# Attention scores over 32 rows per pair of heads, two units side by side, and value products for four pairs at once

## The chip, the cores and the metric

The kernel runs on one core of one Trainium2 chip. The metric is device time of one launch in microseconds (us), lower is better. PE is TensorE, PEld its weight loads, DVE is VectorE, ACT is ScalarE, POOL is GpSimd, SP is the engine that issues most transfers.

## What is computed

The reference is one layer in three parts: cross-attention, a state-space block (convolution, scan over 64 steps, gates) and a feed-forward block with rounded weights and activations. Only the first part is touched:

```python
# x: (16, 64, 256), ctx: (16, 256, 256), 16 heads of 16 columns, mask: (16, 256)
q = layernorm(x) @ Wq * 16 ** -0.5
k, v = split(ctx @ Wkv)
attn = softmax(where(mask, -inf, q_head @ k_head.T))      # per batch row and head
x = x + (attn @ v_head) @ Wproj + bproj
x = x + mamba(layernorm(x))
x = x + ffn(layernorm(x))
```

## The kernel before

The 1024 rows of x are eight tiles of 128 rows, each of two batch rows of 64. All heads are held as columns of two halves `hf` of 128 partitions, eight heads each. While tile t goes through its attention, the keys, queries and values of tile t+1 are made, and the end of tile t-1 (projection, norms) is done. All arithmetic here is float32.

A tile's attention is eight **units** (`UNITS`), and the function `body` of each engine is one pass over steps u = 0 to 7. A unit holds a bank of scores of 128 x 512: two matmuls of 256 columns each. With 64 query rows, a matmul of 128 output rows takes two heads. In the kernel before, unit u belongs to one batch row (`bb = u // 4`) and to two pairs of heads. The pairs are told apart by zeros: `spread_queries` on GpSimd writes `qbd`, in which the 128 rows hold the queries of one head and zeros for the seven others, so that each score matmul contracts over all 128 partitions (`scores`, L456).

A unit's way through the engines:

- TensorE writes its scores to bank u % 2 (`scores`; called at step u-2).
- VectorE adds the mask and takes the maximum (`mask_scores`, L1173, two instructions and two short reads of the accumulator), into one of four buffers `sm`.
- ScalarE takes the exponent (`exps`, L868), VectorE inverts the sums (`invert_sums`, L1180, one step later), GpSimd multiplies (`normalise`, L1596).
- TensorE transposes the probabilities into bank 2 or 3 (`turn_probs`, L465, at step u+1).
- ScalarE copies the even units, VectorE the odd ones, to `pt_sb` (`copy_pt`, L874 and L1185, at step u+3).
- TensorE multiplies with the values (`values`, L481), in `o_ps` with four pairs of heads in four groups of 32 columns of the array.

At step u TensorE first issues the scores of unit u+2, which wait for the mask of unit u (`masked`), so that one bank can be filled while the other is masked. Each engine works through its own list in order; a waiting instruction holds all behind it. The order is the one written in `body`: `PE_KEYS0, PE_KEYS1` and so on are the steps at which TensorE makes the first and second half of the keys (0, 2; L493), the queries (3; L509), the values of both batch rows (4, 5; L520), `project` (3; L530) and `scan_in` (6; L537). VectorE does at step 4 `pick_heads` (L1191, L1195), at step 5 `copy_keys`, `copy_queries`, `make_mask` and `add_proj`, at step 6 `norm_y1`, at step 7 `copy_vals` and `norm_z`. On every even step it copies an odd unit's probabilities.

Three tiles have more to do: in tile 5 ScalarE sums the weights' magnitudes, in tile 6 VectorE rounds the weights (L1273 and others), and in tile 7 it convolves (L1308, L1312) while TensorE does the first products of the next part. Tile 0 builds constants on VectorE at step 6 (L1281, L1282).

Of the kernel before, what the change touches and what calls it, by code (L numbers as in the profile page):

```python
# [45 lines left out]
CON_ID, CON_HEAD, CON_PAR, CON_SEL, CON_M64 = 0, 128, 136, 138, 155  # L46
# [17 lines left out]
LAG_TURN, LAG_VALUES = 1, 2  # L64
# [8 lines left out]
POOL_RSTD0, POOL_BIAS, POOL_RSTD1, POOL_RSTD2, POOL_SPREAD0 = 2, 3, 4, 6, 3  # L73
POOL_SPREAD1 = 5
# [16 lines left out]
def build(nc, x, ctx_t, mask, wq, wkv, wproj, bproj, vecs, cons, win, wall, wout, wg, wu, wd, out):  # L91
    with ExitStack() as ctx:
# [74 lines left out]
        pt_sb = first_use(13312, 2048).rearrange("p (u a q) -> p u a q", u=4, a=4)  # L167
# [6 lines left out]
        qt = first_use(24576, 256).rearrange("p (k t) -> p k t", k=KD)  # L174
# [58 lines left out]
        q_ready, q_sb = sem("q_ready", PE), sem("q_sb", DVE)  # L233
# [4 lines left out]
        qbd_ready = sem("qbd_ready", POOL)  # L238
# [52 lines left out]
        def lagged(tile, u, lag, first, fn, only=None):  # L291
# [4 lines left out]
            if only is None or v % 2 == only:  # L296
                fn(tile if v >= 0 else tile.step(-1), v % UNITS)
# [145 lines left out]
        def _(pe):  # L443
            start(pe, PE)
            def scores(tile, u):
                bb, hf, jj = u // 4, (u // 2) % 2, u % 2
                if u == 0:
                    pe.wait_ge(qbd_ready, count(tile.t * 2 + 2))
                    pe.wait_ge(k_sb[0], count(tile.t + 1))
                if u == 2:  # L450
                    pe.wait_ge(k_sb[1], count(tile.t + 1))
# [17 lines left out]
            def values(tile, u):  # L469

                bb, hf = u // 4, (u // 2) % 2
                if u == 1:
                    pe.wait_ge(v_in_sb[0], count(tile.t + 1))
                    pe.wait_ge(att_ready, count(tile.t))
                if u == 5:
                    pe.wait_ge(v_in_sb[1], count(tile.t + 1))
                pe.wait_ge(pt_in_sb[0], count(tile.t * 4 + (u // 2 + 1)))
# [1269 lines left out]
```

## Time and profile before

| | us |
|---|---|
| three runs | 557.35, 552.49, 557.58 |
| median | 557.35 |
| the profiled execution, its own time | 556.49 |
| its span | 554.7 |
| mean granted clock of TensorE | 0.94 |

In the trace a float32 matmul stands as two instructions (x4 for two matmuls), a transpose as one. The profile gives busy time for each engine, the granted clock of TensorE (1.00 is its full speed), what each instruction waited for, and the chain of work that ended last. The attention takes the span's stretch from 19 us to 226 us.

### The profile page before, as it was taken

How to read it: one execution, taken by the hardware profiler on the slowest of the kernel's cores; microseconds unless marked ns; L12 is line 12 of the kernel's file. 1: busy time of each engine (PE TensorE's matmuls, PEld its weight loads, DVE VectorE, ACT ScalarE, POOL GpSimd, SP SyncE). 2: the span in 40 equal slices, each digit the busy share in tenths (PEclk: the TensorE clock that was granted, in tenths of full speed). 3: DMA queues.
4: the chain of work that ended last, by engine and by line, in shares of the span. 5: the costliest groups of instructions: out<-in, count | busy, mean ns of one | idle time of the engine just before them, and what ended most of it. 6: DMA issues, size and time to landing. Idle time of an engine off the chain costs nothing.

```text
span 554.7 us, 9494 instructions
## 1 busy us (share of the span) xinstructions
PE 465.1 (84%) x3268; PEld 331.8 (60%) x3268; DVE 414.3 (75%) x800; ACT 258.5 (47%) x563; POOL 301.9 (54%) x310
## 2 busy tenths in 40 slices
PE   4999999999999797668796787999799988785463
PEld 2676777877767463346564555577678756462232
DVE  1476766766669797458789988688987799758993
ACT  1346546465754434580373263656772442223331
POOL 0554766648566624047664365689776789401100
PEclk9999999999999798977898898999999999799985
DMA  8910101101000000000000000000000000000000
GB/s 304 382 40 2 39 1 40 38 2 40 2 1 0 2 0 2 1 1 1 0 1 1 0 2 2 1 0 1 1 2 2 1 0 2 0 1 19 21 19 19
DMA packets 5806, 13.76 MB, mean 25 GB/s; under 512 B 768, under 2 KB 3584, under 8 KB 5248
## 3 DMA queue, kind: packets, MB, share of 16 engines
q1 hardware_dynamic: 5200, 12.67, 6.3%
q8 instruction: 26, 0.43, 0.3%
q10 hardware_dynamic: 560, 0.51, 0.3%
q14 instruction: 20, 0.16, 0.1%
HBM read 12.12 MB, written 1.05 MB: 24 GB/s over the span
## 4 chain that ended last, share of the span: by engine, by line
PE 48%; DVE 23%; issue 10%; POOL 8%; ACT 6%; DVEq 0%; ACTq 0%; POOLq 0%
PE ps L456 8%; PE ps L700 6%; PE ps L710 6%; POOL both L1652 5%; DVE both L1341 4%; PE ps L465 4%; PE ps L493 4%; PE ps L520 3%; ACT both L969 3%; PE ps L481 3%; PE ps L728 3%; DVE xc L1312 2%; PE ps L552 2%; PE ps L664 2%; DVE xc L1308 2%
## 5 line engine op out<-in xcount | busy, mean ns | idle before, releaser
L1652 POOL TENSOR_TENSOR both<-both 128x1024 f32<-128x1024 f32 x64 | 152.0, 2388 | 70.3 <-DVE both L1341 70.2
L1341 DVE TENSOR_TENSOR_SCAN both<-both,ps 128x1024 f32<-128x1024 f32 x64 | 145.1, 2280 | 33.8 <-PE ps L710 21.7
L700 PE MATMUL ps<-both 64*128 64x256 f32 x512 | 78.1, 426 | 25.4 <-DVE both L1341 17.8
L868 ACT ACTIVATE both<-both,negmax 128x256 f32<-128x256 f32 x128 | 63.8, 500 | 67.8 <-DVE negmax L1173 67.7
L969 ACT ACTIVATE both<-delta,a_neg 128x504 f32<-128x504 f32 x128 | 79.6, 705 | 25.7 <-DVE both L1341 25.7
L1596 POOL TENSOR_SCALAR both<-both,rden 128x256 f32<-128x256 f32 x128 | 63.3, 508 | 51.2 <-DVE rden L1180 51.2
L710 PE MATMUL ps<-con,both 128*128 128x128 f32 x512 | 75.6, 294 | 3.8 <-POOL both L1652 3.8
L710 PEld LDWEIGHTS ps<-con,both 128*128 128x128 f32 x512 | 59.6, 149 | 26.9 <-issue 19.1
L700 PEld LDWEIGHTS ps<-both 64*128 64x128 f32 x512 | 47.1, 197 | 45.6 <-DVE both L1341 27.8
L456 PE MATMUL ps<-both 128*128 128x256 f32 x256 | 70.1, 397 | 5.0 <-POOL both L1585 3.5
L1173 DVE CUSTOM_DVE_ANT_0 both<-ps,both 128x256 f32<-128x256 f32 x128 | 49.0, 420 | 17.3 <-PE ps L456 16.7
L456 PEld LDWEIGHTS ps<-both 128*128 128x128 f32 x256 | 45.0, 194 | 18.1 <-issue 7.2
L1585 POOL TENSOR_TENSOR both<-both,con 128x1024 f32<-128x1024 f32 x16 | 32.3, 2024 | 26.0 <-DVE both L1150 26.0
L1185 DVE COPY both<-ps 128x512 f32<-128x512 f32 x32 | 21.9, 684 | 25.7 <-PE ps L465 25.7
L465 PE MATMUL ps<-con,both 128*128 128x128 f32 x256 | 39.6, 278 | 1.0 <-ACT both L874 0.6
L465 PEld LDWEIGHTS ps<-con,both 128*128 128x128 f32 x256 | 32.4, 144 | 10.1 <-issue 4.4
L493 PE MATMUL ps<-both 128*128 128x512 f32 x64 | 32.3, 632 | 6.3 <-DMA both<-in_ctx_t 6.3
L520 PE MATMUL ps<-both 128*128 128x256 f32 x128 | 30.1, 379 | 0.0
L982 ACT ACTIVATE both<-ps 128x512 f32<-128x512 f32 x24 | 13.1, 595 | 32.9 <-PE ps L653 32.9
L1657 POOL TENSOR_TENSOR f_s<-f_s,eps 128x1 f32<-128x1 f32 x8 | 1.5, 190 | 49.0 <-DVE f_s L1411 49.0
L520 PEld LDWEIGHTS ps<-both 128*128 128x128 f32 x128 | 24.2, 190 | 3.3
L868 ACT ACTIVATION_READ_ACCUMULATOR both<-both,negmax 128x1 f32 x128 | 24.1, 188 | 0.0
(143 smaller groups left out, 704.3 us busy)
## 6 DMA issues: line engine op xcount, KB each, us to landing
both<-in_ctx_t SPq DMA_DIRECT2D x8, 512.0 KB, 3.3
both<-in_wg SPq DMA_DIRECT2D x1, 1024.0 KB, 10.4
both<-in_wu SPq DMA_DIRECT2D x1, 1024.0 KB, 12.3
both<-in_wd SPq DMA_DIRECT2D x1, 1024.0 KB, 14.3
win_sb<-in_win SPq DMA_DIRECT2D x1, 1024.0 KB, 16.8
resid<-in_x SPq DMA_DIRECT2D x1, 896.0 KB, 8.9
both<-in_wkv SPq DMA_DIRECT2D x1, 512.0 KB, 3.9
both<-in_mask SPq DMA_DIRECT2D x1, 512.0 KB, 6.0
```

The lines of the kernel that those rows point to most:

```text
L456: mm = pe.matmul(bank(u % 2)[:, q * LK:(q + 1) * LK], qbd[:, tile.par, bb, hf, j * P:(j + 1) * P], kt_sb[:, tile.par, hf, bb * LK:(bb + 1) ...
L465: tr = pe.transpose(bank(2 + u % 2)[:, (q * 2 + kt) * P:(q * 2 + kt + 1) * P], sm[:, u % 4, q * LK + kt * P:q * LK + (kt + 1) * P], ident)
L493: mm = pe.matmul(bank(6 - hf), wkv_sb[:, k, hf * P:(hf + 1) * P], ctx_sb[:, tile.par, k], start=k == 0, stop=k == KD - 1)
L520: mm = pe.matmul(bank(5 + bb)[:, kt * D:(kt + 1) * D], ctx_sb[:, tile.par, k, bb * LK + kt * P:bb * LK + (kt + 1) * P], wkv_sb[:, k, D:2 * ...
L700: mm = pe.matmul(out_v[:, :, s], ut[L * r:L * (r + 1), e.idx % 2, 2 * e.tt + s], bd[L * r:L * (r + 1), e.nh, e.tt, s * HN // 2 * L:(s + 1) ...
L710: mm = pe.matmul(bank(4 + e.idx % 2)[:, e.tt * P:(e.tt + 1) * P], h_sb[:, hu % RING_H, n * P:(n + 1) * P], ident, start=False, stop=e.nh = ...
L868: act.activation(s, s, ACT.Exp, scale=-1.0, bias=negmax[:, u % 4, q:q + 1], accum_out=den[:, u % 4, q:q + 1]).then_inc(expd, 1)
L969: act.activation(da[sl % 2].rearrange("p (a n s t) -> p a n s t", a=GT, n=HN, s=2)[:, :, n, :, 1:L], delta[:, idx % RING_X].rearrange("p ( ...
L1173: dve.tensor_tensor_reduce(sm[:, u % 4, q * LK:(q + 1) * LK], bank(u % 2)[:, q * LK:(q + 1) * LK], maskf[:, tile.par, bb * LK:(bb + 1) * L ...
L1341: dve.tensor_tensor_scan(h_sb[:, hu % RING_H], da[e.slot % 2][:, e.tt * HU:(e.tt + 1) * HU], bank(2 * (hu % 2), 2), 0.0, ALU.mult, ALU.add ...
L1596: pool.tensor_scalar(s, s, rden[:, u % 4, q:q + 1], 1.0, ALU.mult, ALU.mult).then_inc(normed, 1)
L1652: pool.tensor_tensor(h, h, cb[:, e.nh, e.tt], ALU.mult).then_inc(g_ready, 1)
```

## The change

- `q2` takes the place of `qbd` and `qt`. VectorE's `copy_queries` is now two instructions instead of one: it writes the queries twice, multiplied once by the parity column of the even heads and once by that of the odd heads (`CON_PAR`). Thus 32 partitions hold one pair of heads, and 64 + 64 columns tell its heads apart. GpSimd's `spread_queries` is gone.
- A score matmul contracts over the 32 partitions of one pair. Unit u is now one pair of heads (of half `hf = u // 4`) with both batch rows; its two matmuls are the two batch rows. `scores` is called for even u alone and issues units u and u+1 together, in turns, in different rows of the array and in banks 0 and 1. It waits until all units below u are masked (`masked`, 2u). Each of both units still has its own `s_ready`, and VectorE masks them one after the other.
- `values` is called twice a tile, for four units at once (16 matmuls instead of four times 8), with a lag of 3 steps instead of 2. `pt_sb` has eight buffers in place of four.
- In tile 6 the matmul for the mean of the weights stands ahead of the scores of that step, not behind them.

```diff
-LAG_TURN, LAG_VALUES = 1, 2
+LAG_TURN, LAG_VALUES = 1, 3
...
-        qbd = first_use(0, 4096).rearrange("p (a b k n) -> p a b k n", a=2, b=2, k=KD)
+        q2 = first_use(0, 1024).rearrange("p (a k b r q) -> p a k b r q", a=2, k=KD, b=2, r=2)
...
             def scores(tile, u):
-                bb, hf, jj = u // 4, (u // 2) % 2, u % 2
+                hf = u // 4
...
-                pe.wait_ge(masked, count(tile.t * 16 + (2 * u - 2)))
-                for q in range(2):
-                    j = 2 * jj + q
-                    mm = pe.matmul(bank(u % 2)[:, q * LK:(q + 1) * LK], qbd[:, tile.par, bb, hf, j * P:(j + 1) * P],
-                                   kt_sb[:, tile.par, hf, bb * LK:(bb + 1) * LK], start=True, stop=True)
-                mm.then_inc(s_ready, 1)
+                pe.wait_ge(masked, count(tile.t * 16 + 2 * u))
+                for bb in range(2):
+                    for v in (u, u + 1):
+                        rows = slice(32 * (v % 4), 32 * (v % 4) + 32)
+                        mm = pe.matmul(bank(v % 2)[:, bb * LK:(bb + 1) * LK],
+                                       q2[rows, tile.par, hf, bb].rearrange("p r q -> p (r q)"),
+                                       kt_sb[rows, tile.par, hf, bb * LK:(bb + 1) * LK], start=True, stop=True)
+                        if bb == 1:
+                            mm.then_inc(s_ready, 1)
...
-                for kt in range(2):
-                    for j in range(4):
-                        mm = pe.matmul(o_ps[32 * j:32 * j + 32, (hf * 2 + bb) * P:(hf * 2 + bb + 1) * P],
-                                       v_sb[:, tile.par, bb, kt, hf * P + 32 * j:hf * P + 32 * j + 32],
-                                       pt_sb[:, u % 4 - 1 + j // 2, j % 2 * 2 + kt], start=kt == 0, stop=kt == 1)
+                for bb in range(2):
+                    for kt in range(2):
+                        for j in range(4):
+                            mm = pe.matmul(o_ps[32 * j:32 * j + 32, (hf * 2 + bb) * P:(hf * 2 + bb + 1) * P],
+                                           v_sb[:, tile.par, bb, kt, hf * P + 32 * j:hf * P + 32 * j + 32],
+                                           pt_sb[hf][:, j, bb * 2 + kt], start=kt == 0, stop=kt == 1)
...
             def copy_queries(tile):
-                dve.tensor_scalar(qt[:].rearrange("p k t -> p (k t)"), bank(6)[:, 0:D], -QSCALE, None, ALU.mult
-                                  ).then_inc(q_sb, 1)
+                for r in range(2):
+                    dve.tensor_scalar(q2[:, tile.par, :, :, r], bank(6)[:, 0:D].rearrange("p (k b q) -> p k b q", k=KD, b=2),
+                                      con[:, CON_PAR + r:CON_PAR + r + 1], -QSCALE, ALU.mult, ALU.mult
+                                      ).then_inc(q2_ready, 1)
...
-            def spread_queries(tile, halves):
-                pool.wait_ge(q_sb, count(tile.t + 1))
-                pool.wait_ge(s_ready, count(tile.t * 8 - 8))
-                for hf in halves:
-                    pool.tensor_tensor(
```

On TensorE, the list from step 0 of a tile in the middle to the queries at step 3 was this (L456 scores, L493 keys, L465 transposed probabilities, L481 values' products, L501 the transposes for the queries, L509 the queries):

```order
L456 MATMUL ps<-both 128x256 x2
L493 MATMUL ps<-both 128x512 x2
L465 MATMUL ps<-con,both 128x128 x4
L456 MATMUL ps<-both 128x256 x2
L465 MATMUL ps<-con,both 128x128 x4
L481 MATMUL ps<-both 32x128 x8
L456 MATMUL ps<-both 128x256 x2
L493 MATMUL ps<-both 128x512 x2
L501 MATMUL ps<-con,both 128x128 x2
L465 MATMUL ps<-con,both 128x128 x4
L456 MATMUL ps<-both 128x256 x2
L509 MATMUL ps<-both 128x128 x4
```

At the same place the changed kernel has this (L453 scores, L492 keys, L464 transposes, L480 values' products; the list begins in front of the pair of steps 0 and 1):

```order
L453 MATMUL ps<-both 128x256 x4
L492 MATMUL ps<-both 128x512 x2
L464 MATMUL ps<-con,both 128x128 x8
L453 MATMUL ps<-both 128x256 x4
L492 MATMUL ps<-both 128x512 x2
L500 MATMUL ps<-con,both 128x128 x2
L464 MATMUL ps<-con,both 128x128 x4
L480 MATMUL ps<-both 32x128 x16
L508 MATMUL ps<-both 128x128 x4
```

The scores of units 2 and 3 stand together in front of the first half of the keys, those of 4 and 5 in front of the second half; the products of the tile before stand two steps later and hold both groups in one.

On VectorE, step 5 of a tile from the reciprocal to the last statistics was this (L1145 keys, L1150 queries, L1161 mask, L1202 to L1128 `add_proj`):

```order
L1180 RECIPROCAL rden<-den 128x2
L1145 COPY both<-ps 128x512
L1150 TENSOR_SCALAR both<-ps 128x256
L1161 TENSOR_SCALAR both<-both 128x512
L1202 TENSOR_TENSOR y<-ps,resid 128x256
```

and is now this:

```order
L1179 RECIPROCAL rden<-den 128x2
L1143 COPY both<-ps 128x512
L1149 TENSOR_SCALAR both<-ps,con 128x4x64 x2
L1161 TENSOR_SCALAR both<-both 128x512
L1201 TENSOR_TENSOR y<-ps,resid 128x256
```

Only the second instruction on the queries is new; nothing on VectorE is moved.

## Rows read from the trace of the kernel before

**Rows 1.** The page, span in 40 slices: TensorE's granted clock in tenths.

```profile
PEclk9999999999999798977898898999999999799985
```

**Rows 2.** Tiles 4 to 7: length, busy PE, PEld, DVE, ACT, POOL, granted clock.

```profile
112.58:135.43 22.85, 22.85 (x172) 17.45 (x168) 15.60 (x61) 12.58 (x41) 14.81 (x26) 1.00 0.07 25
135.43:158.95 23.52, 23.03 (x172) 17.46 (x168) 15.85 (x60) 17.95 (x47) 14.81 (x26) 1.00 0.00 1
158.95:190.61 31.66, 26.27 (x175) 19.21 (x171) 26.68 (x73) 13.01 (x43) 19.43 (x26) 0.91 0.00 1
190.61:226.02 35.41, 30.53 (x183) 18.18 (x180) 25.51 (x68) 16.50 (x44) 11.84 (x23) 0.94 0.00 1
```

**Rows 3.** Chain that ended last, tile 4: start, us, engine and line.

```profile
112.65 1.06 PE ps L456 x4
113.71 1.72 PE ps L493 x4
115.42 0.44 PE ps L465 x4
115.86 0.86 PE ps L456 x4
...
117.16 0.57 PE ps L481 x16
...
122.04 0.89 PE ps L509 x8
122.93 1.07 PE ps L530 x4
...
126.07 1.73 PE ps L520 x8
...
135.50 1.06 PE ps L456 x4
```

**Rows 4.** TensorE in the scan's part: start, us (idle before it).

```profile
300.51 1.77 PE L700 MATMUL ps<-both 64*128 64x256 f32 x8 [3.41 <-DVE both L1341]
...
306.83 1.14 PE L700 MATMUL ps<-both 64*128 64x256 f32 x8
307.89 1.09 PE L710 MATMUL ps<-con,both 128*128 128x128 f32 x8
```

**Rows 5.** VectorE in tiles 3 and 4: start, us (idle before it).

```profile
106.02 0.45 DVE L1132 TENSOR_SCALAR z<-y,meanvar,rstd 128x256 f32<-128x256 f32 x1
...
107.28 0.42 DVE L1173 CUSTOM_DVE_ANT_0 both<-ps,both 128x256 f32<-128x256 f32 x1
...
113.93 0.42 DVE L1173 CUSTOM_DVE_ANT_0 both<-ps,both 128x256 f32<-128x256 f32 x1 [0.70 <-PE ps L456]
...
115.90 0.69 DVE L1185 COPY both<-ps 128x512 f32<-128x512 f32 x1 [1.12 <-PE ps L465]
...
122.73 0.41 DVE L1173 CUSTOM_DVE_ANT_0 both<-ps,both 128x256 f32<-128x256 f32 x1
...
123.07 0.42 DVE L1173 CUSTOM_DVE_ANT_0 both<-ps,both 128x256 f32<-128x256 f32 x1
...
124.08 0.41 DVE L1150 TENSOR_SCALAR both<-ps 128x256 f32<-128x256 f32 x1
...
125.75 0.18 DVE L1128 BATCH_NORM_AGGREGATE meanvar<-stats 128x2 f32<-128x6 f32 x1
```

**Rows 6.** All engines in order of time: first scores, tile 0, turn to tile 7.

```profile
18.99 1.99 PE L456 MATMUL ps<-both 128*128 128x256 f32 x8 [1.01 <-POOL both L1585]
...
35.35 1.90 POOL L1585 TENSOR_TENSOR both<-both,con 128x1024 f32<-128x1024 f32 x1
35.46 1.87 DVE L1281 CAST identb<-con 128x128 bf16<-128x128 f32 x1
...
182.97 1.13 PE L456 MATMUL ps<-both 128*128 128x256 f32 x4 [2.48 <-POOL both L1585]
```

**Rows 7.** Groups by line on VectorE, 20 to 220 us: count, busy, mean ns.

```profile
L1312 DVE SCALAR_TENSOR_TENSOR xc<-xipad,vec,xc 128x512 f32<-128x512 f32 x12 | 9.5, 792 | 0.4
L1273 DVE TENSOR_SCALAR both<-both,winv 128x2048 f32<-128x2048 f32 x3 | 3.8, 1271 | 0.0
```

More of the change, by code:

```diff
@@ L295, in lagged @@
                 return
-            if only is None or v % 2 == only:
+            if only is None or v % UNITS in only:
                 fn(tile if v >= 0 else tile.step(-1), v % UNITS)
@@ L516, in vals @@
                 else:
-                    pe.wait_ge(q_sb, count(tile.t + 1))
+                    pe.wait_ge(q2_ready, count(tile.t * 2 + 2))
                 for kt in range(2):
@@ L567, in body @@
                 for u in range(UNITS):
-                    if u < UNITS - 2:
-                        scores(tile, u + 2)
-                    elif not last:
-                        scores(nxt, u + 2 - UNITS)
                     if weights == "round" and u == 0:
@@ L576, in body @@
                         pe.matmul(bank(7)[:, 0:3], ones[:], wsum[:], start=True, stop=True).then_inc(w_sum, 1)
+                    if u % 2 == 0 and u < UNITS - 2:
+                        scores(tile, u + 2)
+                    elif u % 2 == 0 and not last:
+                        scores(nxt, 0)
                     if not last:
@@ L596, in body @@
                     lagged(tile, u, LAG_TURN, first, turn_probs)
-                    lagged(tile, u, LAG_VALUES, first, values, 1)
+                    lagged(tile, u, LAG_VALUES, first, values, (3, 7))
                     if last:
@@ L611, in _ @@
             scores(t0, 0)
-            scores(t0, 1)
             pe.wait_ge(loaded, N_LOADED)
@@ L620, in _ @@
             for u in range(UNITS, UNITS + LAG_VALUES):
-                lagged(t7, u, LAG_VALUES, False, values, 1)
+                lagged(t7, u, LAG_VALUES, False, values, (3, 7))
             def x_proj(g, c, k, free):
@@ L853, in copy_vals @@
                 act.wait_ge(v_ready[0], count(tile.t + 1))
-                act.wait_ge(pv_done, count(tile.t * 4 - 4))
+                act.wait_ge(pv_done, count(tile.t * 2 - 2))
                 act.activation(v_sb[:, tile.par, 0].rearrange("p k d -> p (k d)"), bank(5), ACT.Copy
@@ L872, in copy_pt @@
                 act.wait_ge(pt_ready, count(tile.t * 8 + (u + 1)))
-                act.wait_ge(pv_done, count(tile.t * 4 + (u // 2 - 1)))
-                act.activation(pt_sb[:, u % 4].rearrange("p a q -> p (a q)"), bank(2), ACT.Copy
+                act.wait_ge(pv_done, count(tile.t * 2 + u // 4 - 1))
+                act.activation(pt_sb[u // 4][:, u % 4].rearrange("p a q -> p (a q)"), bank(2), ACT.Copy
                                ).then_inc(pt_in_sb[0], 1)
@@ L887, in body @@
                     exps(tile, u)
-                    lagged(tile, u, LAG_COPY_EVEN, first, copy_pt, 0)
+                    lagged(tile, u, LAG_COPY_EVEN, first, copy_pt, (0, 2, 4, 6))
                     if not last:
@@ L1004, in _ @@
             for u in range(UNITS, UNITS + LAG_COPY_EVEN):
-                lagged(Tile(0, NT - 1), u, LAG_COPY_EVEN, False, copy_pt, 0)
+                lagged(Tile(0, NT - 1), u, LAG_COPY_EVEN, False, copy_pt, (0, 2, 4, 6))
             copy_gates(0, 2, 5)
@@ L1218, in body @@
                     lagged(tile, u, LAG_INVERT, first, invert_sums)
-                    lagged(tile, u, LAG_COPY_ODD, first, copy_pt, 1)
+                    lagged(tile, u, LAG_COPY_ODD, first, copy_pt, (1, 3, 5, 7))
                     if not last:
@@ L1327, in _ @@
                 lagged(t7, u, LAG_INVERT, False, invert_sums)
-                lagged(t7, u, LAG_COPY_ODD, False, copy_pt, 1)
+                lagged(t7, u, LAG_COPY_ODD, False, copy_pt, (1, 3, 5, 7))
             def scan(hu):
@@ L1610, in body @@
                     normalise(tile, u)
-                    if u == POOL_SPREAD0 and not last:
-                        spread_queries(nxt, [0])
-                    if u == POOL_SPREAD1 and not last:
-                        spread_queries(nxt, [1])
             def pool_resid(tile):
```

53 lines of the change are left out of this document (20 added, 33 removed).

## The prediction

> **What bounds the kernel now.** I read the clock first [rows 1]: apart from a few slices TensorE has its full clock, so its durations can be taken at face value. Then the stretches of the attention [rows 2]: tile 4 takes 22.85 us, and TensorE is busy for all of them, VectorE for 15.60, GpSimd for 14.81. The chain of waits agrees: through this tile it never leaves TensorE, from the scores at 112.65 to the same scores of the next tile at 135.50 [rows 3]. So in tiles 1 to 5 TensorE's list is the bound and nobody else's time counts. Tile 6 is another matter: 31.66 us with TensorE busy for 26.27 and VectorE for 26.68 [rows 2], since VectorE rounds the weights. In tile 7 it convolves. The scan behind 226 us is not touched.
>
> One tile's TensorE list in chain time [rows 3]: scores of a unit 0.86, or 1.06 behind the values' products, since the array's shape changes (four of each: 7.68); products 4 x 0.57 = 2.28; transposes 8 x 0.44 = 3.52; keys 2 x 1.72; queries 0.89; values 2 x 1.73; projection 1.07; the remaining 0.51 are four small transposes. Sum 22.85.
>
> **What TensorE saves.** The trace has no matmul over 32 rows, but the same pattern over 64: four matmuls of 256 columns, in turns on two row groups and two banks (L700). They take 1.06 from start to start (306.83 to 307.89), against 8 x 0.215 = 1.72 one after the other [rows 4]. That is what two row groups side by side give, and I take 1.06 for a pair of units, its change of shape included, plus 0.1 on the instruction in front of it. Ends: 0.96, if the shape costs nothing more, and 1.92, if groups of 32 rows run one after the other. The 128-column weights are still loaded in full. Four pairs cost 4 x 1.16 = 4.64 instead of 7.68. The products are the same matmuls in two visits, 2 x (2 x 0.57 + 0.2) = 2.68 instead of 2.28, and the 0.8 of four shape changes were in the scores' sum. TensorE's list thus becomes about 20.3 us, 2.5 less per tile. If it stayed the bound, five tiles would give 12.7 us.
>
> The Trainium skill (TensorEngine Tiling, Mode switching requires drain) says that changing the tiling mode drains the array; the 0.20 between 1.06 and 0.86 [rows 3] agrees. The same page's PSUM Bottleneck speaks against this change: tiling speeds up TensorE and not the emptying of PSUM, which may become the bound. By its ideal of two tiles at once a pair would take 0.86, which changes the sum below by 0.2 per pair at most. Its warning is my forecast, but the row of VectorE decides that, not the page.
>
> **What the change takes away: the second bank.** Before, the scores of unit u+2 needed only the mask of unit u. Now a pair fills banks 0 and 1 together and waits for both masks of the pair before it. Hence a loop without slack: scores of the pair, mask, VectorE's other work of the even step, mask, scores of the next pair. Queued behind the waiting scores on TensorE are the keys or values of that step and the transposes of the unit before, and VectorE's `copy_pt` of every even step waits for just those transposes. VectorE cannot reach the second mask before. I go round one tile with the durations of the rows. Pieces: first mask 1.2 after the pair starts (113.93 - 112.65 = 1.28, a little less because the first unit's last matmul is not the pair's last); a mask 0.70 until the next instruction and 0.76 to its end (122.73, 123.07 + 0.42); release to TensorE about 0.13, an estimate; transposes 0.60 to their modelled end; `copy_pt` 0.61; another 256-column VectorE instruction 0.33 start to start [rows 3, 5].
>
> - Pair of units 2 and 3 to pair 4 and 5: 1.06 scores, 1.72 keys, 0.60 transposes, 0.04, `copy_pt` 0.61, norm of the next tile 0.33, mask 0.79, release 0.13 = 5.3. TensorE has only 3.8 of work here. VectorE's wait of 1.12 for the transposes is already in the trace (115.90) [rows 5], where it cost nothing.
> - Pair 4, 5 to pair 6, 7: here TensorE has the most to do: 1.06 + 1.72 + 0.22 (two small transposes, half of 0.44) + 0.44 + 0.1 + 1.2 (products) + 0.89 (queries) + 1.07 (projection) + 0.44 + 0.1 = 7.2, and 0.2 for `pick_heads`, which now waits for products that stand two steps later: 7.4. The second mask is done at 6.5, so TensorE is the bound.
> - Pair 6, 7 to pair 0, 1: scores 1.06, values 1.72, transposes 0.60, 0.04, `copy_pt` 0.61, `norm_y1` 1.26 (106.02 to 107.28) [rows 5], mask 0.79, release 0.13 = 6.2. TensorE has 5.4. Step 5 of VectorE (122.73 to 125.75 and 0.21, then 0.33 more for the new query instruction, 3.56) ends 1.85 after the pair's start [rows 5]: later than the scores, but covered by the wait for the transposes. If that cover goes, the 0.33 counts.
> - Pair 0, 1 to pair 2, 3: `norm_z` and `scan_in` come first; scores ready at 1.2, `scan_in` to 1.55, transposes to 2.2, `copy_pt` to 2.8, statistics 0.76 (the 1.26 of `norm_y1` less its norm of 0.45 and the gap behind it), mask 0.79, release 0.13 = 4.5. TensorE has 3.8.
>
> Sum 23.4 against 22.85: **each of tiles 1 to 4 gets about 0.5 us longer**, though TensorE has 2.5 less to do. The 1.5, 0.8 and 0.7 us in which it waits for masks eat that. Bounds for a tile: 20.3 (no wait counts) and 24.6 (scores 0.3 later per pair by an unknown latency).
>
> **The rest.** (a) Start: the first scores waited for GpSimd's two spreads until 18.99 [rows 6]. VectorE now makes q2 in 0.8 us under the values' matmuls, and they start at about 17.8. In tile 0 the constants stand between two masks, which costs, but they get shorter: L1281 (128 x 128) took 1.87 beside a spread of 1.90 [rows 6], and that spread is gone. Going round tile 0 likewise, I reach tile 1's second unit 1.9 us earlier. (b) GpSimd saves 4 us per tile; it is bound by nobody in tiles 1 to 5, so this counts only where scores waited for it, 2.48 at 182.97 [rows 6]. (c) Tile 5: +0.2 for ScalarE's sums. (d) Tile 6: the matmul for the mean is now in front of the scores, and VectorE waits for it before the second mask: +1.2. Then VectorE is the bound with a rounding instruction of 1.27 [rows 7] on every step. On odd steps it hides the latency of the pair, on even steps it lies in the loop. Round the tile I get 6.6 + 7.9 + 8.8 + 7.4 = 30.7 instead of 31.66, the wait of 2.48 being gone. Tiles 5 and 6 together +0.5. (e) Tile 7: the convolutions (3 x 0.79 [rows 7] and more per quarter) keep VectorE busy whatever the scores do: -0.3. (f) Behind it the last transposes and products stand one after the other with twice 16 more instructions, 2 x 0.57 = +1.15, directly in front of `pick_heads` and the next part's first product.
>
> **Sum** on the profiled execution, 556.5: -1.9 + 4 x 0.5 + 0.5 - 0.3 + 1.15 = +1.5, so **558.0 us**, 0.1% above the median of 557.35. 1% is about what a measurement of this kernel can tell from no change (the three runs lie 0.9% apart).
>
> **Rivals.**
> 1. The waits are covered and TensorE's list stays the bound. For it: 15.60 of 22.85 us on VectorE leaves slack, and some of the instructions may be ready sooner than I take them. Against it: the path through keys, transposes and `copy_pt` consists of durations from rows, and nothing in it can be moved. All of it: -12.7 - 1.9 = 542; half: 549. Chance 0.2.
> 2. The clock, slower than before. TensorE now idles in front of every pair. In tile 6 it would idle 2 to 3.5 us each in front of three pairs and in tile 7 for longer. In the trace, tile 6 and its idle 5.4 us have a mean clock of 0.91, tiles 4 and 5, with at most 0.5 idle, 1.00 [rows 2]. In the scan, after an idle of 3.41 us, L700 took 1.77 instead of 1.14 [rows 4]. If the clock falls to its lower level through tile 6, where scores, keys and transposes are now in VectorE's loop, they take twice as long: +3 for the first pair (scores, keys, transposes 3.4), +6.5 for the second (7.2 of TensorE's work against 7.9), +2 and +1 for the others, 12 in all: 570; for half the tile 564. It decides from the point where the idle time in front of a pair reaches that of the scan's row. If it falls in the steady tiles too, more. Chance 0.18.
> 3. Groups of 32 rows don't run side by side, so the change doesn't do what it says. A pair then takes 1.92 in place of 1.06, on the loop in all four intervals: 0.86 x 4 x 5 = 17, and some 2 in tile 0 and 6: 577. Against it: L700 does it with 64 rows. Chance 0.07.
> 4. My forecast, masks and transposes give the saving back: 552 to 563. Chance 0.5. The remaining 0.05 goes to worse chains of waits.
>
> The Trainium skill (TensorE: Matmul & The Clock Gate, HAM oscillation) puts a fall to half the clock down to idle stretches between bursts of matmuls, which is rival 2; 1.77 against 1.14 behind the idle 3.41 us agrees [rows 4].
>
> **Range.** 546 to 570 takes in the forecast, the likelier half of rival 1 and rival 2 up to its full price; it leaves out rival 3 and the full rival 1. Faster by over 1% (under 551.8): 0.22. Within 1%: 0.51. Slower by over 1% (over 562.9): 0.27.
>
> **What the profile would show.** If I am right: in tiles 1 to 4 the scores' group has a pair of 8 instructions in 1.14 us; TensorE's idle time in front of L453, ended by VectorE's mask, is 1.5, 0.8 and 0.7 per tile and none in front of units 6 and 7; a period of 23.0 to 23.8; VectorE still waits about 1.1 for the transposes on even steps; the chain goes to and fro between TensorE and VectorE. If rival 1: a period under 22 and hardly any idle time in front of L453. If rival 2: PEclk at 0.8 or less over tiles 6 and 7. If rival 3: a pair of 1.9 us. I am wrong if VectorE masks a first unit much later than 1.2 us after the pair's start, or if a period ends on ScalarE or GpSimd, which I took as never late (they have 12.58 and about 10.8 us of work in 23).

## The result and the profile after

The changed kernel takes 566.2 us (median of 4 runs, 565.06 to 567.65) against 557.47 for the kernel before (4 runs, 552.49 to 559.19). The ratio is 1.0178, interval 1.0131 to 1.0225: 1.8% slower. The forecast was 558.0, its range 546 to 570. The profiled execution took 565.44 us, with a span of 563.4 us. Ratios here and below are formed without slow runs (one of four in experiment 2 and one of four in experiment 6, each over 1.5% above the fastest of its kernel), while the medians are of all runs.

The page of the changed kernel (busy time of the engines, the granted clock in 40 slices, three groups by line):

```profile
PE 455.6 (81%) x3261; PEld 313.4 (56%) x3268; DVE 414.0 (73%) x808; ACT 258.9 (46%) x563; POOL 271.9 (48%) x294
PEclk9796989999898988877999889799989999898897
L453 PE MATMUL ps<-both 32*128 32x256 f32 x256 | 39.8, 430 | 27.3 <-DVE negmax L1172 27.3
L1172 DVE CUSTOM_DVE_ANT_0 both<-ps,both 128x256 f32<-128x256 f32 x128 | 49.1, 421 | 25.6 <-PE ps L453 24.9
L1184 DVE COPY both<-ps 128x512 f32<-128x512 f32 x32 | 22.0, 686 | 36.0 <-PE ps L464 35.8
```

The scores now stand in 256 instructions over 32 rows. What they waited for were the masks of the pair before them: 27.3 us of idle TensorE. VectorE's copy of the transposed probabilities waited 35.8 us for TensorE. The clock row is the other half of the story. In [rows 1] almost every slice of the attention reads 9; here there is a 7 in the second slice, a 6 in the fourth and 8s in others.

The stretches of tiles 0 to 6 of the changed kernel, each from the scores of units 2 and 3 to the same scores of the next tile (length, then busy PE, PEld, DVE, ACT, POOL, then the granted clock), which answer to [rows 2]:

```profile
21.25:47.16 25.91, 23.23 (x127) 15.30 (x127) 15.00 (x57) 11.93 (x41) 9.23 (x20) 0.77 0.27 104
47.16:72.80 25.64, 22.81 (x170) 15.65 (x169) 15.58 (x61) 11.98 (x40) 10.79 (x24) 0.90 0.07 22
72.80:97.95 25.15, 22.11 (x168) 15.09 (x168) 15.77 (x62) 12.57 (x42) 11.22 (x24) 0.93 0.07 22
97.95:121.29 23.34, 20.41 (x168) 14.57 (x168) 15.70 (x62) 12.59 (x42) 11.18 (x24) 1.00 0.07 23
121.29:144.63 23.34, 20.41 (x169) 14.57 (x169) 15.70 (x62) 12.58 (x42) 11.18 (x24) 1.00 0.08 25
144.63:170.88 26.25, 22.26 (x170) 15.43 (x171) 16.47 (x65) 17.99 (x48) 11.07 (x24) 0.93 0.01 1
170.88:202.64 31.76, 25.06 (x168) 16.68 (x168) 25.28 (x70) 13.11 (x44) 15.45 (x24) 0.84 0.01 1
```

Tiles 3 and 4 show the change alone, at full clock: TensorE's list is 20.41 us, 2.4 shorter than before, and yet the tile takes 23.34 us, 0.49 more. Tiles 1 and 2 do the same work at a clock of 0.90 and 0.93 and take 2.3 and 1.8 us more than that. Tile 5, which has ScalarE's sums besides, takes 2.9 more at 0.93.

One round of the loop in tile 3 (all engines in order of time: start, length; idle time before it and its releaser in brackets), with the four pairs of this tile and the first of the next (the last row is cut by the end of the view):

```profile
97.95 1.13 PE L453 MATMUL ps<-both 32*128 32x256 f32 x8 [0.72 <-DVE negmax L1172]
...
99.02 1.98 PE L492 MATMUL ps<-both 128*128 128x512 f32 x4
99.30 0.42 DVE L1172 CUSTOM_DVE_ANT_0 both<-ps,both 128x256 f32<-128x256 f32 x1 [1.32 <-PE ps L453]
...
100.84 1.04 PE L464 MATMUL ps<-con,both 128*128 128x128 f32 x8
...
101.47 0.69 DVE L1184 COPY both<-ps 128x512 f32<-128x512 f32 x1 [1.32 <-PE ps L464]
102.17 0.41 DVE L1130 TENSOR_SCALAR both<-resid,meanvar,rstd 128x256 f32<-128x256 f32 x1
102.50 0.42 DVE L1172 CUSTOM_DVE_ANT_0 both<-ps,both 128x256 f32<-128x256 f32 x1
...
103.42 1.13 PE L453 MATMUL ps<-both 32*128 32x256 f32 x8 [1.54 <-DVE negmax L1172]
...
104.48 1.98 PE L492 MATMUL ps<-both 128*128 128x512 f32 x4
...
110.47 0.87 DVE L1149 TENSOR_SCALAR both<-ps,con 128x256 f32<-128x256 f32 x2
...
110.76 1.13 PE L453 MATMUL ps<-both 32*128 32x256 f32 x8
...
114.29 0.69 DVE L1184 COPY both<-ps 128x512 f32<-128x512 f32 x1 [0.63 <-PE ps L464]
...
117.03 1.13 PE L453 MATMUL ps<-both 32*128 32x256 f32 x8 [0.61 <-DVE negmax L1172]
...
121.29 0.92 PE L453 MATMUL ps<-both 32*128 32x256 f32 x6 [0.73 <-DVE negmax L1172]
```

Read it as a circle: the pair (1.07 to the keys at 99.02), the keys, the transposes at 100.84, VectorE's copy at 101.47 for which VectorE has idled 1.32, the norm, the second mask at 102.50, and only then the next pair at 103.42, for which TensorE has idled 1.54. The two engines wait for each other in turn. The gaps between pairs are 5.47, 7.34, 6.27 and 4.26, together 23.34.

TensorE in tiles 0, 2 and 5, at the places where its clock fell to the lower level (1.2 in place of 2.4 GHz); the pair of 1.13 us still ran at the full clock, the keys behind it did not:

```profile
21.25 1.97 PE L453 MATMUL ps<-both 32*128 32x256 f32 x8 [2.56 <-DVE negmax L1172]
23.16 3.78 PE L492 MATMUL ps<-both 128*128 128x512 f32 x4
...
78.26 1.13 PE L453 MATMUL ps<-both 32*128 32x256 f32 x8 [1.54 <-DVE negmax L1172]
79.32 3.68 PE L492 MATMUL ps<-both 128*128 128x512 f32 x4
...
150.09 1.13 PE L453 MATMUL ps<-both 32*128 32x256 f32 x8 [1.54 <-DVE negmax L1172]
151.16 3.64 PE L492 MATMUL ps<-both 128*128 128x512 f32 x4
```

The keys behind the second pair take 3.68 us in tile 2 and 1.98 in tile 3 (104.48), behind the very same wait of 1.54. So behind the same wait the clock fell in one tile and not in the other, and one fall costs 1.7 us here.

**Where the time went.** From the profiled executions, changed less before: tile 0 +3.1, tiles 1 and 2 +5.1, tiles 3 and 4 +1.0, tile 5 +2.7, tile 6 +0.1, tile 7 with its end -0.2. Together +11.8 by the first `pick_heads` of the end (226.02 before, 237.85 after). The span grew by 8.7 only: the scan and what follows, whose code is unchanged, took 3.1 less. That part is not steady. From the first products on `u_sb` to the end it took 318.9 in the kernel before, 315.8 in the changed one, and between 314.5 and 320.2 in the twelve experiments.

### The profile page after: what moved, and what is told of

Read it like the earlier page. It is cut to its first block, busy times and chain, and to the rows that moved or that the text cites. A ratio compares the mean times of both kernels' runs of the same rounds, so it can differ in the third digit from the quotient of the medians.

```text
span 563.4 us, 9447 instructions
## 1 busy us (share of the span) xinstructions
PE 455.6 (81%) x3261; PEld 313.4 (56%) x3268; DVE 414.0 (73%) x808; ACT 258.9 (46%) x563; POOL 271.9 (48%) x294
## 4 chain that ended last, share of the span: by engine, by line
PE 31%; DVE 23%; issue 9%; ACT 6%; POOL 5%; DVEq 0%; another core or an unknown queue 0%; ACTq 0%; POOLq 0%
PE ps L708 6%; PE ps L698 6%; POOL both L1634 4%; DVE both L1340 4%; PE ps L551 3%; ACT both L967 2%; DVE xc L1311 2%; PE ps L492 2%; PE ps L726 2%; PE ps L662 2%; DVE xc L1307 2%; DVE f_s L1462 2%; DVE both L1172 1%; PE ps L377 1%; PE ps L453 1%
## 5 line engine op out<-in xcount | busy, mean ns | idle before, releaser
L1583 POOL TENSOR_SCALAR both<-both,rden 128x256 f32<-128x256 f32 x128 | 65.2, 522 | 71.5 <-DVE rden L1179 71.5
L698 PE MATMUL ps<-both 64*128 64x256 f32 x512 | 76.6, 420 | 27.7 <-DVE both L1340 19.3
L708 PEld LDWEIGHTS ps<-con,both 128*128 128x128 f32 x512 | 57.8, 146 | 25.8 <-issue 17.2
L1172 DVE CUSTOM_DVE_ANT_0 both<-ps,both 128x256 f32<-128x256 f32 x128 | 49.1, 421 | 25.6 <-PE ps L453 24.9
L453 PE MATMUL ps<-both 32*128 32x256 f32 x256 | 39.8, 430 | 27.3 <-DVE negmax L1172 27.3
L1184 DVE COPY both<-ps 128x512 f32<-128x512 f32 x32 | 22.0, 686 | 36.0 <-PE ps L464 35.8
L492 PE MATMUL ps<-both 128*128 128x512 f32 x64 | 41.9, 793 | 6.2 <-DMA both<-in_ctx_t 6.2
L453 PEld LDWEIGHTS ps<-both 32*128 32x128 f32 x256 | 24.7, 197 | 36.8 <-issue 26.6
L464 PE MATMUL ps<-con,both 128*128 128x128 f32 x256 | 40.8, 289 | 0.4 <-POOL both L1583 0.4
L464 PEld LDWEIGHTS ps<-con,both 128*128 128x128 f32 x256 | 32.4, 149 | 13.8 <-issue 7.2
L1566 POOL TENSOR_TENSOR vareps<-meanvar,eps 128x1 f32<-128x1 f32 x24 | 6.3, 263 | 60.6 <-DVE meanvar L1126 60.5
L519 PE MATMUL ps<-both 128*128 128x256 f32 x128 | 30.8, 385 | 0.0
L492 PEld LDWEIGHTS ps<-both 128*128 128x128 f32 x64 | 14.3, 245 | 24.2 <-issue 24.2
L519 PEld LDWEIGHTS ps<-both 128*128 128x128 f32 x128 | 23.1, 190 | 4.9 <-issue 2.3
```

What stands on the lines that cost most here:

```text
L453: mm = pe.matmul(bank(v % 2)[:, bb * LK:(bb + 1) * LK], q2[rows, tile.par, hf, bb].rearrange("p r q -> p (r q)"), kt_sb[rows, tile.par, hf ...
L464: tr = pe.transpose(bank(2 + u % 2)[:, (q * 2 + kt) * P:(q * 2 + kt + 1) * P], sm[:, u % 4, q * LK + kt * P:q * LK + (kt + 1) * P], ident)
L492: mm = pe.matmul(bank(6 - hf), wkv_sb[:, k, hf * P:(hf + 1) * P], ctx_sb[:, tile.par, k], start=k == 0, stop=k == KD - 1)
L519: mm = pe.matmul(bank(5 + bb)[:, kt * D:(kt + 1) * D], ctx_sb[:, tile.par, k, bb * LK + kt * P:bb * LK + (kt + 1) * P], wkv_sb[:, k, D:2 * ...
L698: mm = pe.matmul(out_v[:, :, s], ut[L * r:L * (r + 1), e.idx % 2, 2 * e.tt + s], bd[L * r:L * (r + 1), e.nh, e.tt, s * HN // 2 * L:(s + 1) ...
L708: mm = pe.matmul(bank(4 + e.idx % 2)[:, e.tt * P:(e.tt + 1) * P], h_sb[:, hu % RING_H, n * P:(n + 1) * P], ident, start=False, stop=e.nh = ...
```

## The experiments

These are twelve experiments on eleven kernels (7 and 13 are the same one); there is no number 5. Their ratios are against runs of the kernel before on the same chip. Each trace is of one execution.

**1. Only the pairing of the waits** (from the kernel before: scores still over 128 rows, but two units at a time).

```diff
-                pe.wait_ge(masked, count(tile.t * 16 + (2 * u - 2)))
+                pe.wait_ge(masked, count(tile.t * 16 + 2 * (u - u % 2)))
...
+                    if u % 2 == 0 and u < UNITS - 2:
+                        scores(tile, u + 2)
+                        scores(tile, u + 3)
```

> The kernel before, with one part of the change alone: two units' scores (still over 128 rows, one after the other) are issued together and wait for both masks of the pair before. Values, q and GpSimd's spread stay as before. Theory A (the second bank is what the change gives up: a loop of scores, mask, copy of the transposes, mask): the loop has 1.92 us of scores in place of 1.06, so a steady tile takes about 25.5 us instead of 22.85, and the run about 572 us (568 to 578). Theory B (the loss comes from the 32-row form and its changes of shape, the masks are covered): a steady tile stays within 0.3 of 22.85 and the run at 556 to 559.

Measured: 589.76 us (587.71 to 591.87), ratio 1.0594 [1.0564, 1.0624]. A steady tile of this kernel:

```profile
101.24:128.22 26.98, 23.40 (x169) 17.71 (x169) 16.21 (x61) 12.58 (x42) 14.88 (x27) 1.00 0.06 20
```

26.98 us at full clock instead of 22.85, with no more than 23.40 of work on TensorE. Giving up the alternation of the two banks costs 4.1 us a tile when the scores are not made cheaper, more than the 25.5 expected. In this tile TensorE waited 3.3 us for masks, 0.9 for VectorE's copies and 0.5 for `pick_heads`. The run as a whole was forecast at 572 and missed that by 18 us: five tiles of 4.1 are 21 of the 33 us it lost, and the rest, in tiles 0, 6 and 7, was not followed up.

**2. Only the narrow scores** (from the changed kernel: the 32-row scores unit by unit on every step, each waiting for the mask two units back).

```diff
-                pe.wait_ge(masked, count(tile.t * 16 + 2 * u))
+                pe.wait_ge(masked, count(tile.t * 16 + 2 * u - 2))
...
-                    for v in (u, u + 1):
+                    for v in (u,):
...
-                    if u % 2 == 0 and u < UNITS - 2:
+                    if u < UNITS - 2:
                         scores(tile, u + 2)
```

> The changed kernel with the second bank given back: the 32-row scores are issued unit by unit at every step, waiting for the mask two units back, so that no two row groups work side by side (each unit 0.86 us and a change of shape of its own). Theory A: TensorE hardly waits for masks any more, its clock stays full in tiles 1 to 5, and its list, now 8 x 1.06 and some 0.1 each in front, bounds a tile at 24.2 to 24.9 us; the run 562 to 568 us, by work and not by waits. Theory B (the shape changes make the loss): the same list, but dearer than the changed kernel by twice its shape changes, 570 us and more, and waits for masks where they are now.

Measured: 564.89 us (560.79 to 570.21), ratio 1.0122 [1.0072, 1.0172]. A steady tile:

```profile
94.47:118.95 24.48, 24.48 (x169) 16.92 (x168) 15.98 (x61) 12.71 (x41) 11.05 (x25) 1.00 0.07 23
```

TensorE is busy for all of the 24.48 us: it is the bound, the waits are gone, and so is the saving. The gain in TensorE's list comes entirely from two row groups running at once, and that is what needs the pair.

**3. Work for TensorE's idle time** (the changed kernel, with matmuls that go nowhere ahead of the scores of steps 0, 2 and 6).

```diff
+FILL = {0: 1, 2: 3, 6: 1}
...
+                    for _ in range(FILL.get(u, 0)):
+                        pe.matmul(bank(4)[:, 256:512], ident, wkv_sb[:, 0, 0:256], start=True, stop=True)
```

> The changed kernel with matmuls added that compute nothing of use (128 x 256 into the unused half of bank 4): one in front of the score pairs of steps 0 and 6, three in front of that of step 2, 0.43 us each, in the places where TensorE waits for VectorE. No wait and nothing else is changed. Theory A with the clock (the idle stretches let the granted clock fall in tiles 0, 1, 2 and 5, which costs 3 us each): the clock stays at 1.00 through tiles 1 to 5, each takes 23.3 to 23.5 us, and the run is 557 to 560 us, faster than the changed kernel by 6 to 9 though it does more. Theory C (the long tiles 1, 2 and 5 have another cause, for example transfers or ScalarE's sums): they stay at 25 to 26 us and the run at 566 or above.

Measured: 560.66 us (558.64 to 564.29), ratio 1.0078 [1.0041, 1.0115]. Tiles 0 to 6:

```profile
22.31:48.16 25.85, 23.09 (x137) 15.46 (x137) 14.91 (x58) 11.43 (x39) 8.90 (x19) 0.87 0.23 88
48.16:71.50 23.34, 22.57 (x178) 16.15 (x179) 15.69 (x62) 12.58 (x42) 11.22 (x24) 1.00 0.08 25
71.50:94.98 23.48, 22.58 (x178) 16.15 (x179) 15.78 (x62) 12.58 (x42) 11.27 (x24) 1.00 0.07 24
...
141.68:166.28 24.60, 22.87 (x180) 16.37 (x180) 16.48 (x65) 17.99 (x48) 11.12 (x24) 1.00 0.01 2
166.28:196.51 30.23, 25.79 (x178) 17.81 (x178) 25.39 (x70) 13.12 (x44) 15.49 (x24) 0.89 0.00 1
```

With 2.2 us more work per tile TensorE holds its full clock in tiles 1 to 5, and these take 118.1 us instead of 123.7. So 5.6 us of the loss were the clock, and the loop of tiles 1 to 4 stays at 23.3 to 23.5 whether TensorE idles in it or not. Against the kernel before, whose tiles 1 to 5 took 114.9, the 3.2 us that are left are the loop itself.

**4, 6 and 10. Breaking the loop.** The copy waits for transposes that stand behind the scores and the keys. Run 4 puts the transposes ahead of the scores on even steps:

```diff
+                    if u % 2 == 0:
+                        lagged(tile, u, LAG_TURN, first, turn_probs)
                     if u % 2 == 0 and u < UNITS - 2:
                         scores(tile, u + 2)
...
-                    lagged(tile, u, LAG_TURN, first, turn_probs)
+                    if u % 2 == 1:
+                        lagged(tile, u, LAG_TURN, first, turn_probs)
```

> The changed kernel with one thing moved: on even steps the transposes of the unit before stand ahead of the score pair instead of behind the keys or values, so that the copy on VectorE that stands between the two masks finds them done. Theory A (the path pair, keys, transposes, copy, mask is the loop): the intervals of 5.3 and 6.2 us shrink to about 3.9 and 5.5, a steady tile takes 21.1 us (20.8 to 21.8), TensorE is nearly always busy and keeps its clock, and the run takes 549 us (545 to 553), below both kernels. Theory D (the transposes are no cover but wait themselves for GpSimd, and hold up the scores behind them): a tile stays above 23 us and the run at 564 or more.

Measured: 565.67 us (561.64 to 567.17), ratio 1.0149 [1.0112, 1.0187]. A miss: 549 and a tile of 21.1 were expected. Tile 2, the one at full clock, took 22.69 us, 0.65 less than in the changed kernel; its two neighbours took 24.3 to 24.4 at a clock of 0.93. In tile 2:

```profile
71.89 0.67 DVE L1187 COPY both<-ps 128x512 f32<-128x512 f32 x1
...
73.33 0.55 POOL L1572 TENSOR_TENSOR rstd<-vareps,neg_half 128x1 f32<-128x1 f32 x1
...
73.99 0.41 DVE L1133 TENSOR_SCALAR both<-resid,meanvar,rstd 128x256 f32<-128x256 f32 x1 [1.44 <-POOL rstd L1572]
...
75.24 1.13 PE L453 MATMUL ps<-both 32*128 32x256 f32 x8 [1.42 <-DVE negmax L1175]
```

The copy waits for nothing now, but the norm behind it waits 1.44 us for GpSimd's 1/sqrt, which had been hidden behind the wait for the transposes. One wait took the place of the other, in the same loop. Run 6 also makes the 1/sqrt a step earlier, and run 10 makes that second move alone:

```diff
-POOL_RSTD0, POOL_BIAS, POOL_RSTD1, POOL_RSTD2 = 2, 3, 4, 6
+POOL_RSTD0, POOL_BIAS, POOL_RSTD1, POOL_RSTD2 = 1, 3, 4, 6
```

> The kernel with the transposes first, and the next tile's 1/sqrt on GpSimd one step earlier (step 1 instead of 2, ahead of a normalisation), because with the transposes out of the way VectorE waited 1.44 us between the two masks of step 2 for this value. Theory A (a chain of single late values between two masks; each that is taken away shows the next): the interval from pair 2, 3 to pair 4, 5 falls from 5.47 to about 3.95 us, then TensorE's own work bounds most of the tile, 21.2 us (20.9 to 21.8) at full clock; TensorE is busy for 96% of it, so the clock stays at 1.00 in tiles 1 to 5; the run 551 us (546 to 556), below both kernels. Theory E (at these gaps the clock falls anyway): tiles of 22.5 to 24 us with the clock at 0.93, and 558 or more.

> The changed kernel with only the second move of the fast version: the next tile's 1/sqrt on GpSimd at step 1 instead of 2, the transposes where the change has them. If the copy behind the transposes is what is last between the two masks (Theory A), taking away a wait that isn't last gives nothing: a steady tile stays at 23.34 us (23.2 to 23.5) at full clock, and the run at 562 to 568. If the two moves gain independently: about 22.3 and 557 to 561.

Measured: both moves 548.31 us (541.78 to 549.97), ratio 0.9825 [0.9725, 0.9925]; the second alone 561.26 (one run, with the kernel before at 556.92). A steady tile of run 6, then one of run 10:

```profile
89.51:110.82 21.31, 20.71 (x168) 14.43 (x169) 15.46 (x62) 12.58 (x42) 11.18 (x24) 1.00 0.08 25
```

```profile
91.62:114.86 23.24, 20.41 (x169) 14.57 (x169) 15.60 (x62) 12.59 (x42) 11.18 (x24) 1.00 0.07 23
```

With both moves the tile takes 21.31 us, TensorE being busy for 20.71: near its list. The second move alone leaves 23.24. So of the 2.03 us that both moves give, the first alone gives 0.65 and the second alone 0.10: the two waits lie one behind the other. In run 6 the clock holds 1.00 in tiles 1 to 5 as well, in whose first four TensorE idles for 0.6 us each.

**7 and 13. Filler at the ends** (run 6 with matmuls that go nowhere in tiles 0, 6 and 7, where its clock was still 0.86 and 0.88).

```diff
+                    for _ in range(({0: 4, 6: 4} if first else {0: 2, 2: 4, 6: 2} if weights == "round" else {0: 2} if last else {}).get(u, 0)):
+                        pe.matmul(bank(4)[:, 256:512], ident, wkv_sb[:, 0, 0:256], start=True, stop=True)
```

> The kernel before this one, plus matmuls that compute nothing of use, only where TensorE waits in tile 0 (four each at steps 0 and 6), tile 6 (two, four and two at steps 0, 2 and 6) and tile 7 (two at step 0). If the clock is what is left of the loss there: tile 0 shrinks by 2 to 3 us (21.3 to 45 us), tile 6 by about 1, the run by 3 to 4 against the kernel without them: 547 to 548. If those tiles are bound by VectorE alone: no difference beyond 1 us, or a loss where the matmuls stand in the way.

> The best version once more (the changed kernel with both moves and matmuls that compute nothing of use in tiles 0, 6 and 7), on the same chip as the kernel before with the moves. Theory A: 542 to 544, and 4 to 5 us below that run, from five tiles of 21.3 in place of 22.75 us less a tile 6 and 7 that gain less. Theory B: the two agree within 1 us.

Measured: 542.84 us (539.4 to 543.1), ratio 0.9769 [0.9715, 0.9822], and on another chip 545.64 (543.23 to 546.35), ratio 0.9801 [0.9753, 0.985]. This is the fastest version. It gained more than the 3 to 4 us expected: 5.5 against run 6 on the same chip. Tile 0 of the second:

```profile
22.19:43.48 21.29, 19.91 (x138) 14.10 (x138) 14.91 (x58) 11.29 (x39) 8.85 (x19) 1.00 0.30 115
```

It took 24.04 us in run 6. By the first `pick_heads` of the end run 7 is 3.9 us ahead of run 6 (214.68 for 218.58), 3.0 of them by the start of tile 1.

**8 and 9. Is the loop really VectorE's?** One more 128 x 256 VectorE instruction on every even step, in run 3's kernel (8) and in the kernel before (9).

```diff
+                    if u % 2 == 0:
+                        dve.tensor_tensor(xc[:, 4, 0:D], wkv_sb[:, 0, 0:D], wkv_sb[:, 1, 0:D], ALU.add)
```

> The kernel with filler matmuls everywhere (clock at 1.00, steady tiles of 23.34 us), with one more VectorE instruction of 0.34 us (a sum of two 128 x 256 pieces that nobody reads) between the two masks of every pair, four times a tile. Theory A: VectorE's time between two masks is on the path in three of four intervals and partly in the fourth (TensorE-bound, by way of the projection): a steady tile becomes 24.4 to 24.7 us, though VectorE is busy for only 15.7 of 23.3 us. Theory B (VectorE has slack, the masks are covered): it stays at 23.3 to 23.5.

> The kernel before the change with the same additional VectorE instruction in the same four places of a tile. Theory A: two banks give slack, TensorE is the bound, and a steady tile stays at 22.85 us (22.8 to 22.9). Theory B has no reason for a difference between this kernel and the changed one: the same, 0 or 1.4 us, in both.

Measured, one run each: 567.34 us and 563.08. A steady tile of the first, then one of the second:

```profile
98.13:122.59 24.46, 22.58 (x178) 16.14 (x178) 17.15 (x66) 12.59 (x42) 11.42 (x24) 1.00 0.07 23
```

```profile
118.28:142.71 24.43, 23.06 (x172) 17.45 (x168) 18.62 (x65) 12.39 (x41) 15.33 (x26) 1.00 0.07 23
```

The changed loop grows by 1.12 for 1.45 us of added VectorE work (17.15 - 15.70), as expected. But the kernel before grew too, by 1.58, where none was expected. VectorE got the same four instructions, yet its busy time rose by 3.0, to 18.62. Its trace shows why:

```profile
135.19 2.07 POOL L1587 TENSOR_TENSOR both<-both,con 128x1024 f32<-128x1024 f32 x1
135.42 1.99 DVE L1132 TENSOR_SCALAR z<-y,meanvar,rstd 128x256 f32<-128x256 f32 x1
...
139.57 0.40 DVE L1132 TENSOR_SCALAR xn<-z,meanvar,rstd 128x256 f32<-128x256 f32 x1
...
140.03 0.44 PE L537 MATMUL ps<-con,xn 128*128 128x128 f32 x2 [1.10 <-DVE xn L1132]
```

The added work pushed a norm beside GpSimd's spread, where it took 1.99 us instead of 0.45 [rows 5], and TensorE then waited for the next one. So run 9 does not show that the kernel before has no slack for VectorE work; it shows that such work can be moved into a collision.

**11 and 12. Do the moves need the change?** The kernel before with both moves (11), and with filler in tiles 6 and 7 as well (12: four matmuls at step 6 and two at step 0, where run 7 has two, four and two in tile 6, two in tile 7 and eight in tile 0). In run 12 the filler overwrites the attention output of two head groups of tile 6, which the kernel before keeps in that half of the bank; the work done is otherwise the same.

```diff
-POOL_RSTD0, POOL_BIAS, POOL_RSTD1, POOL_RSTD2, POOL_SPREAD0 = 2, 3, 4, 6, 3
+POOL_RSTD0, POOL_BIAS, POOL_RSTD1, POOL_RSTD2, POOL_SPREAD0 = 1, 3, 4, 6, 3
...
+                    if u % 2 == 0:
+                        lagged(tile, u, LAG_TURN, first, turn_probs)
                     if u < UNITS - 2:
...
-                    lagged(tile, u, LAG_TURN, first, turn_probs)
+                    if u % 2 == 1:
+                        lagged(tile, u, LAG_TURN, first, turn_probs)
```

> The kernel before the change with both moves of the fast version (transposes ahead of the scores on even steps, the 1/sqrt one step earlier). Theory A: TensorE's list of 22.85 us bounds its steady tiles, and the moves take nothing out of it: 22.85 us a tile and a ratio to before of 0.995 to 1.005; the gain of the fast version then is the saving of the 32-row scores set free. Rival (the two moves help any version): 21.5 to 22.5 us a tile, and 550 us or less.

> The kernel before with the transposes ahead of the scores on even steps and 1/sqrt one step earlier (as in the run before_both_moves), and with matmuls that compute nothing of use in tile 6 (4 of 256 columns ahead of the scores of its step 6) and tile 7 (2 at step 0), where TensorE waits. It asks whether the change is still worth something once both kernels have the same moves and the same help for the clock. Theory A (TensorE's list bounds the kernel before at 22.75 us a tile, the changed one at 21.3): about 547.5, so 4 to 5 us above the best version. Theory B (what the best version gained came from the moves and the clock, none from the change): within 1 us of the best version, 543.

Measured: 548.61 us (547.23 to 550.2), ratio 0.9854 [0.9816, 0.9893], and 552.65 (548.42 to 556.47), ratio 0.993 [0.9897, 0.9963]. Run 11, a steady tile and tile 6:

```profile
89.18:111.93 22.75, 22.46 (x170) 17.41 (x169) 15.64 (x61) 12.82 (x41) 14.98 (x26) 1.00 0.07 24
...
158.13:188.29 30.16, 25.17 (x172) 18.42 (x171) 27.20 (x75) 13.09 (x44) 21.51 (x26) 0.94 0.01 1
```

The steady tile gained only 0.1, as expected, for TensorE's list is its bound. That the kernel as a whole gained 8 us was not expected (a ratio of 0.995 to 1.005 was). Of the 6.3 by which its span is shorter than that of [rows 2]'s execution, 0.8 come up to tile 6, 1.5 in tile 6 (30.16 for 31.66), 1.4 in tile 7, and 2.6 in the unchanged scan, whose length differs by as much among kernels anyway. The filler of run 12 did no good: 552.65 where 547.5 was expected, and a ratio above run 11's. In tile 6 it only filled its wait (0.19 left of 1.96, and the scores no earlier, 23.16 us after the tile's start in both); in tile 7 it stood ahead of scores that waited for nothing. Later in tile 7 four input projections took 3.78 us at 211.97, where run 11's took 1.98: the clock was at its lower level in spite of it. That trace is of the slowest of run 12's ten runs, so it does not show why the others were slow.

This changes what the moves are worth to the change. With both moves and no filler in either, run 6 stands at 0.9825 [0.9725, 0.9925] and run 11 at 0.9854 [0.9816, 0.9893]: no difference clear of noise. In the traces the steady tile is 1.44 us shorter (22.75 to 21.31), but run 6 begins tile 1 3.2 us later (46.89 for 43.69), its clock in tile 0 being 0.86 where run 11's is 1.00. By the first `pick_heads` of the end it is 3.7 us ahead (218.58 for 222.30). With filler at the ends, the changed kernel's 0.9769 and 0.9801 stand beside the same 0.9854, some 4 us. On the one chip that ran both, run 13 is 7 us faster than run 12, but run 12 is not the best form of the kernel before. So the change shortens the steady tile once its loop is opened. For the whole kernel that is under 1%, with help for the clock that did not suit the other kernel, and at the edge of what these runs can tell.

## Why the prediction was right or wrong

- **The bound before, TensorE's list:** right. Run 11's moves, which take waits from VectorE, gave a steady tile 0.1 only.
- **TensorE's saving:** right. Its busy time per tile is 20.41 against the 20.3 worked out (the terms as written add up to 20.21), a pair 1.07 to the next instruction against 1.06 taken from [rows 4]. Rival 3 is out. The Trainium skill's warning (TensorEngine Tiling, PSUM Bottleneck) came true as an outcome; by the rows the masks did not get slower (421 ns for an instruction of L1172 against 420 for L1173 before), they only lost the second bank to work in.
- **The loop of the pairs:** right, gap by gap. Forecast 5.3, 7.4, 6.2, 4.5, measured 5.47, 7.34, 6.27, 4.26; sum 23.4 against 23.34, in which errors of up to 0.24 in single gaps partly cancel. Waits 1.5, 0.8, 0.7 against 1.54, 0.61, 0.73. The members of the circle are shown, not only argued: run 4 took the transposes out, run 6 the 1/sqrt behind them, and the tile fell to 21.31; run 8 put VectorE work in and it rose. What the prediction did not see is the 1/sqrt, second in line. It said of the path that nothing in it could be moved, against rival 1. Moving two things in it gave 2.0 us per tile.
- **(a), the start:** the step that failed, the largest error of all. The first scores did start at 17.57, against 17.8 forecast, and the cast that took 1.87 us beside the spread [rows 6] took 0.22. But the second pair then waited 2.56 at 21.25 and ran, with the keys behind it, at the lower clock. Tile 1 began 3.15 us later than before, not 1.9 earlier. This is an error of 5 us. The clock is not all of it: in run 7, with both moves, filler and a clock of 1.00 in tile 0, tile 1 began at 43.88, which is 0.1 earlier than before and still not 1.9.
- **The clock in the steady tiles, rival 2:** the mechanism was named, its place wrong. The prediction let the clock decide only where TensorE idles as long as in the scan's row, 3.41 us, and so put the fall in tiles 6 and 7. It was low in tiles 1, 2 and 5 behind waits of 1.54 us and, from tile 0 into tile 1, of 2.64. Run 3 gives it 5.6 us over tiles 1 to 5. In tile 6, where 12 us were put on it, it was lower too (0.84), but the tile took 31.76 against 30.7 forecast: 1 us.
- **(c), (d), tiles 5 and 6:** +2.8 against +0.5. Of tile 5's +2.7 the clock is 1.65: at full clock, in run 3, it took 24.60, still 1.1 more than before, where the forecast had 0.2 for ScalarE's sums. The +0.5 itself does not follow from the prediction's terms: 30.7 for 31.66 in tile 6, with 0.2 in tile 5 and the loop's 0.5 beside it or not, add up to between -0.8 and -0.3, and the whole sum to at most +0.7 instead of +1.5. The slip happens to lie towards the result.
- **(e), (f), tile 7 and the end:** -0.2 against +0.85 together. Which of the two was too dear was not tried.
- **`copy_queries`:** its second instruction was covered, as forecast: the copy behind it still waited 0.63 us for the transposes (114.29).

So the forecast's own case, within 1% and at most 563, did not come. The sum of its terms was 1.5, the profiled execution gave 8.95: +5 at the start, +4 in tiles 1 to 4, +2.3 in tiles 5 and 6, -1 at the end, and -3 in the scan, for which no term stood and whose cause stays open. The 566.2 lie within 546 to 570, but high in it, where the prediction had put rival 2 for tiles 6 and 7. The clock cost its time at the start and in tiles 1, 2 and 5, so that the range held is in part luck.

## What to carry to other kernels

When a change trades a free buffer for a shorter list, walk the circle buffer, reader, the reader's other work, release, with the rows' durations: here that gave the tile to 0.1 us and its single gaps to 0.25. Then, before calling it fixed, ask for each member what it would wait for if the wait before it were gone; two waits in line show up as one, and removing either alone gains little (here 0.65 and 0.10 of 2.03 us). And count each new idle of TensorE twice, once as time and once as a risk to its clock: here, over tiles 1 to 5, the longer loop took 3.2 us and the clock 5.6.

## What the runs showed of the hardware

- The clock falls behind short waits, and not every time: three waits of about 1.5, 0.6 and 0.7 us in a tile whose TensorE is busy for 20.4 of 23.3 us left it at 1.00 in tiles 3 and 4 and not in tiles 2 and 5. In run 10 tile 4 was hit (0.93, 24.93 us for 23.24). With filler, 22.6 us of work in the same loop, it held 1.00 in tiles 1 to 5. The Trainium skill (TensorE: Matmul & The Clock Gate, HAM oscillation) puts such falls down to idle stretches between bursts, in its own case stretches longer than the bursts. The trace agrees in part: filling the waits kept the clock (run 3), but waits much shorter than the work between them were enough for a fall. No run here shows what makes one tile fall and the next one not.
- Two groups of 32 rows side by side cost the same as two groups of 64: four matmuls of 256 columns (eight instructions in the trace) in 1.07 and 1.06 us. One group at a time, the array's list grows to 24.48 us per tile (run 2), more than the 22.85 of scores over 128 rows.
- A VectorE instruction of 0.4 us took 1.99 beside a 128 x 1024 elementwise product on GpSimd, both ending within 0.15 us of each other (135.19 + 2.07, 135.42 + 1.99). In the kernel before a cast of 128 x 128 took 1.87 us beside such a product [rows 6], and 0.22 in the changed kernel, which has none.
